# Rows for an embedding tower gathered into two buffers, their groups turned earlier in each tile

## The reference

```python
e = jnp.stack([tbl_0[ids[:, 0]], ..., tbl_26[ids[:, 26]]], axis=1)   # 2048 x 27 x 128
interactions = jnp.einsum('bfd,bgd->bfg', e, e)                      # 27 x 27 a sample
flat = interactions[:, triu_i, triu_j]                               # 351 pairs
h = jnp.concatenate([e.reshape(B, -1), flat, dense_ctx], axis=1)     # 3456 + 351 + 16
h = jnp.maximum(h @ W_top1 + b_top1, 0.0)                            # 512
h = jnp.maximum(h @ W_top2 + b_top2, 0.0)                            # 256
y = h @ W_top3                                                       # 1
```

## Time and profile before

| | us |
|---|---|
| median of 3 runs (576.96 to 578.21) | 578.11 |
| span of the profiled execution, first to last instruction | 708.0 |
| TensorE matmul busy in it | 574.9 |
| GpSimd busy in it | 416.2 |
| VectorE busy in it | 347.6 |
| ScalarE busy in it | 232.3 |

### The profile page before, as it was taken

How to read it: one execution, slowest core, us unless ns; L and a number is a source line. 1 busy time by engine, 2 the same in 40 slices (tenths; PEclk the granted TensorE clock), 3 DMA queues, 4 the chain that set the end, 5 groups by cost and what they waited for, 6 DMA issues and landing times.

```text
span 708.0 us, 7882 instructions
## 1 busy us (share of the span) xinstructions
PE 574.9 (81%) x2578; PEld 504.6 (71%) x2578; DVE 347.6 (49%) x1140; ACT 232.3 (33%) x703; POOL 416.2 (59%) x450
## 2 busy tenths in 40 slices
PE   2606688989889898959959896897968979698898
PEld 1505577868778787948848795786857868697786
DVE  4305462819264563808337281554707355372755
ACT  4204423324251513315232331514315161323441
POOL 6775565666666565665746667365664666556001
PEclk9956899989989998989989899799987999989999
DMA  6613411111111111111111111011110111111000
GB/s 211 217 52 110 131 45 44 46 46 44 45 45 50 41 49 41 48 45 39 47 29 50 44 42 52 27 49 42 46 52 26 49 41 49 42 41 46 12 1 1
DMA packets 19581, 37.84 MB, mean 53 GB/s; under 512 B 7780, under 2 KB 8804, under 8 KB 19540
## 3 DMA queue, kind: packets, MB, share of 16 engines
q0 software_dynamic: 13824, 28.34, 15.1%
q1 hardware_dynamic: 5716, 8.99, 4.0%
HBM read 37.30 MB, written 0.01 MB: 53 GB/s over the span
## 4 chain that ended last, share of the span: by engine, by line
PE 59%; another core or an unknown queue 20%; DVE 8%; issue 6%; ACT 5%; DMA 1%; SPq 0%; ACTq 0%; DVEq 0%
PE ps_acc L298 12%; PE ps_acc L299 11%; PE ps_acc L300 11%; PE ps_gram L323 10%; DVE g_buf L666 6%; PE ps_acc L356 6%; PE ps_t L269 5%; PE ps_gram L400 3%; ACT g_buf L582 2%; DVE emb_x L645 1%; DMA g_buf<-in_W_top 1%; ACT emb_x L534 1%; ACT h_t L571 1%; PE ps_gram L352 1%
## 5 line engine op out<-in xcount | busy, mean ns | idle before, releaser
L242 POOL DMA_INDIRECT emb<-in_tbl,idx x405 | 385.8, 953 | 233.4 <-issue 109.4
L298 PE MATMUL ps_acc<-w_hi,emb_x 128*128 128x512 f32 x432 | 211.1, 489 | 28.7 <-DVE emb_x L645 26.6
L645 DVE TENSOR_TENSOR emb_x<-ps_t,emb_x 128x512 fp32r<-128x512 f32 (+1 forms) x111 | 73.9, 667 | 249.6 <-ACT emb_x L534 165.2
L299 PE MATMUL ps_acc<-w_lo,emb_x 128*128 128x512 f32 x432 | 182.7, 423 | 0.0
L300 PE MATMUL ps_acc<-w_hi,emb_x 128*128 128x512 f32 x432 | 181.0, 419 | 0.0
L666 DVE COPY g_buf<-ps_gram 32x112 f32<-32x112 f32 x480 | 129.8, 270 | 93.6 <-PE ps_gram L323 63.1
L323 PE MATMUL ps_gram<-emb_x 128*128 128x224 f32 x480 | 99.5, 335 | 79.2 <-DVE emb_x L645 41.2
L298 PEld LDWEIGHTS ps_acc<-w_hi,emb_x 128*128 128x128 f32 x432 | 131.9, 305 | 35.3 <-DVE emb_x L645 28.0
L323 PEld LDWEIGHTS ps_gram<-emb_x 128*128 128x128 f32 x480 | 83.4, 231 | 102.0 <-DVE emb_x L645 45.1
L582 ACT ACTIVATE g_buf<-ps_gram 32x112 f32<-32x112 f32 x480 | 122.2, 255 | 99.0 <-PE ps_gram L323 64.8
L534 ACT ACTIVATE emb_x<-ps_t 128x512 fp32r<-128x512 f32 (+1 forms) x111 | 63.1, 583 | 272.7 <-PE ps_t L269 137.4
(11 more groups left out here) (61 smaller groups left out, 163.2 us busy)
## 6 DMA issues: line engine op xcount, KB each, us to landing
g_buf<-in_W_top SPq DMA_DIRECT2D x27, 256.0 KB
emb<-in_tbl,idx POOLq DMA_INDIRECT x405
w_cols<-in_W_top SPq DMA_DIRECT2D x1, 512.0 KB
w<-in_W_top SPq DMA_DIRECT2D x1, 512.0 KB
emb<-in_tbl,idx_first POOLq DMA_INDIRECT x27
w_cols<-in_W_top SPq DMA_DIRECT2D x1, 222.0 KB
idx<-in_ids SPq DMA_DIRECT2D x1, 216.0 KB, 4.9
ctx_rows<-in_dense_ctx SPq DMA_DIRECT2D x4, 32.0 KB
```

What stands on the lines that cost most here:

```text
L242: pool.indirect_dma_start(out=emb[:, f * D:(f + 1) * D], out_offset=None, in_=tables[f], in_offset=bass.IndirectOffsetOnAxis(ap=rows, axis ...
L298: pe.matmul(acc, emb_part(0, f), w_hi[:, f, :], start=(f == 0), stop=False)
L299: pe.matmul(acc, emb_part(0, f), w_lo[:, f, :], start=False, stop=False)
L645: dve.tensor_tensor(group_part(1, g), turned_bank(n, g), group_part(0, g).bitcast(fp32), ALU.subtract).then_inc(s_emb_lo, 1)
```

## The change

`emb` gets two halves, and tile t uses half t % 2, with semaphores of its own for each half and group. A gather of tile t then waits for the turn of the same group in tile t-2. In tiles 1 to 14 TensorE's order up to the first unit becomes: products of group 0, turn 2, products 1, turn 3, turn 4, products 2, turn 5, turn 6, `turn_columns`, products 3, `multiply_columns`, two features, `turn_h1`, two features. The first and last tiles keep their order. ScalarE takes the columns and the hidden layer behind all seven splits. VectorE splits group 1 ahead of `turn_blocks`, group 2 ahead of `add_parts` and the first packing, and groups 3 and 4 ahead of the second packing and `layer_3`. In the diff, ScalarE's lines stand ahead of VectorE's, at its end; the branch for tile 0, left out there, holds the order of before.

```diff
-        emb = sb("emb", [P, NF * D])
+        emb = sb("emb", [P, 2, NF * D])
...
+        def rows_of(t, f):
+            return emb[:, t % 2, f * D:(f + 1) * D]
+        def landed(t, g, count):
+            return 16 * (t // 2 * len(GROUPS[g]) + count)
...
-                    if t > 0:
-                        pool.wait_ge(s_pe_t, NG * (t - 1) + g + 1)
+                    if t > 1:
+                        pool.wait_ge(s_pe_t, NG * (t - 2) + g + 1)
...
-                pe.wait_ge(s_gather[g], (t + 1) * 16 * len(GROUPS[g]))
+                pe.wait_ge(s_gather[t % 2][g], landed(t, g, len(GROUPS[g])))
...
                 turn_group(t, 3)
-                multiply_group(t, 2)
-                if t > 0:
+                if t == 0:
...
+                else:
+                    turn_group(t, 4)
+                    multiply_group(t, 2)
+                    turn_group(t, 5)
+                    turn_group(t, 6)
                     turn_columns(t - 1)
-                turn_group(t, 4)
-                if t > 0:
+                    multiply_group(t, 3)
                     multiply_columns(t - 1)
-                multiply_group(t, 3)
-                turn_group(t, 5)
-                if t > 0:
+                    for _ in range(2):
+                        multiply(t, f)
+                        f += 1
                     turn_h1(t - 1)
-                f = 4 * GF
-                for _ in range(GF if t == 0 else 2):
-                    multiply(t, f)
-                    f += 1
-                turn_group(t, 6)
...
                     split_group(t, g)
-                    if t > 0 and g == 3:
-                        take_columns(t - 1)
-                    if t > 0 and g == 4:
-                        relu_h1(t - 1)
-                    if t > 0 and g == 5:
-                        take_h1(t - 1)
+                if t > 0:
+                    take_columns(t - 1)
+                    relu_h1(t - 1)
+                    take_h1(t - 1)
...
-                        if g == 0:
+                        if g == 1:
                             turn_blocks(t - 1)
-                        if g == 1:
+                        if g == 2:
                             add_parts(t - 1)
                             pack_pairs(t - 1, 0, 10)
-                        if g == 2:
+                        if g == 4:
                             pack_pairs(t - 1, 10, NF - 1)
                             if t > 1:
                                 layer_3(t - 2)
```

More of the change, by code:

```diff
@@ L107, in dlrm_tower_kernel @@
         s_w_late = sem("s_w_late")
-        s_gather = [sem(f"s_gather{g}") for g in range(NG)]
+        s_gather = [[sem(f"s_gather{half}_{g}") for g in range(NG)] for half in range(2)]
         s_gather_last = sem("s_gather_last")
@@ L234, in _ @@
                 for g in range(NG):
-                    if t > 0:
-                        pool.wait_ge(s_pe_t, NG * (t - 1) + g + 1)
+                    if t > 1:
+                        pool.wait_ge(s_pe_t, NG * (t - 2) + g + 1)
                     for f in GROUPS[g]:
-                        landed = s_gather[g]
+                        arrived = s_gather[t % 2][g]
                         if t == TILES - 1 and f == NF - 1:
-                            landed = s_gather_last
+                            arrived = s_gather_last
                         rows = idx_first[:, f:f + 1] if t == 0 else idx[:, t, f:f + 1]
                         pool.indirect_dma_start(
-                            out=emb[:, f * D:(f + 1) * D], out_offset=None, in_=tables[f],
+                            out=rows_of(t, f), out_offset=None, in_=tables[f],
                             in_offset=bass.IndirectOffsetOnAxis(ap=rows, axis=0)
-                        ).then_inc(landed, 16)
+                        ).then_inc(arrived, 16)
             pool.wait_ge(s_cols_t, TILES - 1)
@@ L268, in turn_group @@
                 for i, f in enumerate(GROUPS[g]):
-                    last = pe.transpose(turned_bank(n, g)[:, :, i], emb[:, f * D:(f + 1) * D],
+                    last = pe.transpose(turned_bank(n, g)[:, :, i], rows_of(t, f),
                                         ident[:, :])
@@ L275, in turn_last_group @@
                 g, n = NG - 1, NG * t + NG - 1
-                pe.wait_ge(s_gather[g], 16 * ((t + 1) * len(GROUPS[g]) - 1))
+                pe.wait_ge(s_gather[t % 2][g], landed(t, g, len(GROUPS[g]) - 1))
                 pe.wait_ge(s_emb_lo, n - 1)
                 for i, f in enumerate(GROUPS[g][:-1]):
-                    last = pe.transpose(turned_bank(n, g)[:, :, i], emb[:, f * D:(f + 1) * D],
+                    last = pe.transpose(turned_bank(n, g)[:, :, i], rows_of(t, f),
                                         ident[:, :])
@@ L285, in turn_last_feature @@
                 pe.wait_ge(s_emb_lo, NG * t + NG - 1)
-                pe.transpose(last_feature_bank(), emb[:, (NF - 1) * D:NF * D],
+                pe.transpose(last_feature_bank(), rows_of(t, NF - 1),
                              ident[:, :]).then_inc(s_pe_t, 1)
@@ L449, in _ @@
             for t in range(TILES - 1):
+                f = 4 * GF
                 multiply_group(t, 0)
@@ L453, in _ @@
                 turn_group(t, 3)
-                multiply_group(t, 2)
-                if t > 0:
+                if t == 0:
[3 more added lines that the diff above has]
+                    turn_group(t, 5)
+                    for _ in range(GF):
+                        multiply(t, f)
+                        f += 1
+                    turn_group(t, 6)
+                else:
+                    turn_group(t, 4)
+                    multiply_group(t, 2)
+                    turn_group(t, 5)
+                    turn_group(t, 6)
                     turn_columns(t - 1)
-                turn_group(t, 4)
-                if t > 0:
+                    multiply_group(t, 3)
                     multiply_columns(t - 1)
-                multiply_group(t, 3)
-                turn_group(t, 5)
-                if t > 0:
+                    for _ in range(2):
+                        multiply(t, f)
+                        f += 1
                     turn_h1(t - 1)
-                f = 4 * GF
-                for _ in range(GF if t == 0 else 2):
-                    multiply(t, f)
-                    f += 1
-                turn_group(t, 6)
                 for k in range(UNITS):
```

## The result

| | before | after |
|---|---|---|
| median of 4 runs, us | 577.54 (575.81 to 578.21) | 581.27 (580.99 to 581.48) |
| ratio to before, 95% interval | | 1.0072 [1.0058, 1.0086] |
| profiled execution, us | 576.53 (a new profile, see below) | 581.37 |
| its span, us | 574.7 | 579.5 |

The change makes the kernel slower by 0.7%. The forecast was 582.0.

A forecast was written before the change was run, and what follows sets the result against it. TensorE's lane was taken to bound the kernel, gathers close behind. A loss of 7.9 us in tile 1, less 0.3 a tile from the columns, gave +4.0 on 578.1: 582.0 us forecast, range 573.0 to 586.5.

The forecast's parts named there:

- What bounds before: Whole kernel: TensorE's 34.0 us a tile bounds, gathers close at 33.7; nearly all 130 us of profile excess is late TensorE signals and clock.
- The sum of before: Kernel before: tile 1's products at 53.2, its units at 74.3, tile 14's at 516.3, end at 571.2 us.
- Buffers 0: Gathers on GpSimd: two buffers free them from turns already past, so worth 0.
- Turns early: TensorE, tile 1: turns 4, 5, 6 wait 4.0, 1.5, 3.3 us for gathered rows; units at 82.2, loss 7.9, once.
- Columns later: TensorE, 14 tiles: group 3's products hide the columns' wait for ScalarE's copy, saving 0.3 us a tile, to 33.7.
- +4.0: Units of tile 14 at 520.3 us after the change against 516.3 before, the forecast's net loss.
- Splits ahead of packing 0: VectorE: second packing and `layer_3`'s addition end 0.6 us before `turn_columns` wants them; cost 0, bound above 0.5 a tile.
- Clock 0 to 3: TensorE's clock: three waits may halve it, a loss of 0 to 3 us; 0 taken, as products break the waits.
- Quick gathers: Rival, GpSimd: gathers quicker in timed runs, at 0.95 us each giving 574 to 575 us; chance 0.20.
- Late signals or buffers: Rival: late signals or gathers' waits occur in timed runs too, so turn 6 and buffers pay, 570 to 576 us; chance 0.10.
- Packing late: Rival, VectorE: its chain overruns by 0.5 us a tile, 7 more, 586 to 589 us; chance 0.07.
- It cancels: Rival: tile 0 ends 2 to 3 us later than summed, giving the gathers that lead, 578 to 580 us; chance 0.20.

The follow-up runs named there:

- before again: The unchanged kernel before, profiled a second time because its first profile was of a disturbed execution: 576.53 us, span 574.7 us.
- before with fewer gathers: The kernel before with the gather of feature 25 left out in tiles 2 to 15 (26 instead of 27): 577.38 us, ratio 1.0005.
- columns later: The kernel before with only `multiply_columns` moved behind group 3's products and `turn_h1` behind two features, one buffer: 574.21 us, ratio 0.9943.
- the loads later: The changed kernel with SyncE's late weight and bias loads, not the dense rows, issued only when turn 6 of tile 1 is done: 585.41 us.
- with fewer gathers: The changed kernel with the gather of feature 25 left out in tiles 2 to 15 (26 instead of 27): 577.78 us, ratio 1.0005 to before.
- turn 6 put back: The changed kernel with turn 6 just ahead of the last two features before the units, ScalarE's columns and hidden layer behind split 5: 580.76 us, ratio 1.0065.
- the product cut short: The changed kernel with turn 6 moved back late and VectorE's W_top3 product over 8 of 256 numbers in all tiles but the last: 580.82 us.

## Why the prediction held, step by step

**What bounds before: right.** The profile's 130 us of late signals were not the kernel's (before again), and the kernel without them is TensorE's lane with the gathers close behind (before with fewer gathers: no gain; columns later: gain, until the gathers are met). The tile of 34.0 is 33.92. The gathers' 33.7 is 33.86 in after (the last gather of tile 4 is issued at 173.54, that of tile 14 at 512.14): the pace of the earlier trace rows is that of most gathers in every profile; what it left out is that some take 1.0 to 1.8 us.

**The sum of before: one piece missing.** It came to 571.2 with 6.9 for what lies around the span. The span is 574.7 and 1.8 lie around it. Nearly all that is missing is in tile 0, where I put the products of tile 1 at 53.2; they start at 57.41. TensorE of before again in order of time:

```profile
41.72 0.83 PE L323 MATMUL ps_gram<-emb_x 128*128 128x224 f32 x6
...
49.17 1.11 PE L269 MATMUL ps_t<-ident,emb 128*128 128x128 f32 x4 [2.02 <-DMA emb<-in_tbl,idx]
...
50.51 0.63 PE L299 MATMUL ps_acc<-w_lo,emb_x 128*128 128x512 f32 x1
...
57.41 0.61 PE L298 MATMUL ps_acc<-w_hi,emb_x 128*128 128x512 f32 x1 [1.94 <-DVE emb_x L645]
```

Turn 0 of tile 1, between the units, waits 2.02 us for rows that come late, and what follows runs slower (0.63 for a product that takes 0.40 elsewhere; the granted clock from 41 to 55 is 0.88). The unit stage takes 13.5 us instead of 10.1. The experiment with the loads later shows what delays the rows: without those loads the stage is back at 10.1 and the products start at 54.16.

**Buffers 0: right.** 1.0008 [0.9995, 1.0021]. GpSimd waits for no turn in after, as said.

**Turns early: right in kind, too large in size.** The term was 4.0 + 1.5 + 3.3 us of waits and a loss of 7.9. The waits are 0.46 + 1.50 + 3.02, the loss 6.2. What failed is the start it was taken from: with tile 1 at 57.8 and not at 53.2, turn 4 nearly finds its rows. The working also left out what the waits do to the clock (below), so the 6.2 are made of waits that were put too high and a clock that was put at nothing: 5.0 of waits, some 1.5 of clock, 0.4 for the later start of the products, less the columns' 0.4, come near it (6.5). With the loads out of the way, turn 6 is issued 19.7 us behind group 0's products (54.16 to 73.90), where 10.5 would do without waits: 9.2 lost, against 8.8 in the working. That is near by luck, though: the waits are 2.45 and 3.10, turn 5 has none, and some 3 us are products at half the clock (those of groups 0 and 2 take 4.5 us each, where 3.0 are usual). The loss of that kernel against a before without the late loads was not measured, as the columns of before need them sooner.

That the loss comes "once" is shown by the runs: with fewer gathers it stays alone, and with tile 1 in the old order tile 2 pays it. What the prediction gave as its mark, waits for gathers in tile 1 only, was too strict. TensorE's list of waits in after (total us, times, longest):

```profile
PEld ps_t L277 <- DMA emb<-in_tbl,idx: 12.1, 13, 3.3
PE ps_t L277 <- DMA emb<-in_tbl,idx: 8.9, 8, 3.0
```

Five of the 8.9 us are the three of tile 1; the rest are turn 0 of tile 1, late as in before, and short waits in later tiles, one of 0.87 at 345.86. The list of the weight loads, which come ahead of the matmuls, is fuller: behind tile 1 it has nine waits, at turn 6 of every tile from 5 to 14 but tile 10, 0.16 to 1.11 us long and 3.8 in sum. That is what the 13 tiles take above 33.5 each (3.7).

**Columns later: the gain was there, the gathers took it.** I put it at 0.3 a tile. Alone it gives 0.25 (33.92 to 33.67) and in the new order TensorE could run at 33.5, 0.42 less. After gets 0.13 of that in the mean, since the gathers' 33.86 binds from tile 4 on. So the second term, 13 x 0.3 = 3.9, was too large by 2.2, and the first by 1.7. That is why +4.0 came out as +4.5 at the units of tile 14: two errors of size nearly cancel, and the closeness of 582.0 to 581.27 is in part luck.

**Splits ahead of packing 0, right.** The new order with the rows there takes 33.5 in every tile, so neither VectorE nor ScalarE holds it above that. In tile 2 of after, VectorE's second packing ends at 108.6 and the addition of `layer_3` at 108.96; `turn_columns` starts at 109.40 without a wait. The slack is 0.4 where 0.6 was worked out.

**Clock 0 to 3: a part of it came.** The clock in windows of after (busy us by engine, then clock, DMA share, GB/s):

```profile
65.00:74.00 9.00, 4.28 (x20) 3.72 (x20) 3.37 (x19) 1.64 (x3) 6.73 (x7) 1.00 0.20 51
74.00:85.00 11.00, 10.94 (x40) 9.03 (x41) 0.56 (x1) 2.24 (x5) 8.51 (x9) 0.84 0.20 55
```

and of the kernel with the loads later, twice ahead of turn 4, and from turn 4 to turn 6:

```profile
54.00:59.00 5.00, 4.83 (x15) 4.06 (x16) 4.28 (x3) 0.00 (x0) 3.78 (x5) 0.66 0.19 52
59.00:64.00 5.00, 3.74 (x20) 3.42 (x17) 3.31 (x14) 1.19 (x2) 3.78 (x5) 1.00 0.15 39
65.00:74.00 9.00, 5.71 (x21) 4.54 (x22) 2.66 (x18) 1.19 (x2) 6.72 (x8) 0.81 0.18 51
```

In after the clock stays full through the waits and drops behind them, to a mean of 0.84 over 11 us (0.51 from 74 to 76, close to the lower of its two levels, 1.2 GHz). From turn 6 to the first unit tile 1 takes 11.06 us (74.06 to 85.12), tile 5, at full clock, 9.61 (210.03 to 219.64): the clock costs some 1.5 us here. It is part of the 6.2. The rule of the Trainium skill that was weighed, TensorE: Matmul & The Clock Gate, Part 1, that the clock falls after idleness, agrees with this window: the 2 us put beside it were nearer than my 0.

**The rivals.** Quick gathers: no, the pace is the same in the timed kernels, since leaving one out of 27 moves after and not before. Late signals or buffers: no. Packing late: no. "It cancels" named the right place, tile 0 ending later than the sum has it, but its reason (a later start gives the gathers a lead) covers only part of it. The products of tile 1 started 4.6 us later than in the sum, but the rows of group 6 came 1.6 later too (74.06 for 72.5), and the clock took 1.5, so a loss of 6.2 was left.

## What to carry to other kernels

Ahead of moving a consumer earlier, set the time of its data's arrival beside its new place in the order, tile by tile: here the rows could not come sooner, and the wait that the move made was paid once and never earned back. A second buffer pays only where the trace shows the producer waiting for a release. And the part of the change that removes time from the binding engine is worth trying alone: it gave 0.6%, while the whole change lost 0.7%.

## What the runs showed of the hardware

- A profiled execution can be far from the timed ones: 708.0 us of span against 574.7 for the same kernel, with the late signals of the earlier trace rows and the clock of the earlier trace rows behind them. What caused it is open.
- With late weight loads of 1.5 MB on SyncE's queue, a gather's way from issue to landing has a median of 4.8 us, and 2.5 in the one run that has these loads later.
- A gather's issue on GpSimd takes 0.94 us, but up to 1.15 when it begins while `layer_3`'s product runs on VectorE; with the product cut from 0.42 to 0.17 us it takes 0.94 again. What counts, by the starts that the profile gives, is which begins first: in before again, after and turn 6 put back, the 35 long gathers that met the product began while it had more than 0.15 us to go, and ended 0.81 to 0.83 us behind its end; seven that began ahead of it, and three that began in its last 0.1 us, kept 0.94 or 0.95. (The cut product has at most 0.1 us to go where a gather meets it.)
- In the four profiles where they were counted (these three and the product cut short), every long gather from tile 1 on ran beside an instruction of VectorE that reads two tensors from SBUF: the packing, the addition of parts, that product, or, for one early gather of tile 1, the split of the weights. Not every gather beside such an instruction was long. With turn 6 put back, of those that ran beside a split (105, which reads one of its tensors from PSUM) or a copy of blocks (150) none was long. The Trainium skill, SBUF — State Buffer, section "SBUF: two separate sides", says that a VectorE instruction with two inputs in SBUF and a GpSimd instruction that reads SBUF lock the same pair of ports against each other, and that whichever starts first has it for its whole length. The counts and the order of starts agree with it. A lock for the whole length of a gather is not seen: products that began inside one still took 0.42 to 0.43 us. Only the product was tested; the other instructions were not taken apart.
